# Window attention on one core: three output tiles finished in one step, one exponential a step earlier, one key tile on VectorE, the input load behind the value spreading

## The chip, the core and the metric

The kernel runs on one core of one Trainium2 chip. The time is the device time of one whole execution in microseconds (us), and the median of several runs is compared. TensorE (PE in the profile), VectorE (DVE), ScalarE (ACT), GpSimd (POOL) and SyncE (SP, which here only issues DMAs) each run their own queue strictly in order and wait for each other through semaphores.

## The reference

```
x = x + L0(_gn(x))     # input (16, 56, 56, 192); _gn: mean and variance over a group of 6 channels
x = x + L1(_gn(x))

L0: a = softmax((x @ W_attn + b_attn) as (6 heads, 9 taps)); v = x @ W_v + b_v
    y = sum over the 9 taps of the 3x3 patch of v * a;  return y @ W_proj + b_proj
L1: roll by (-3, -3), cut into 7x7 windows (8 rows of 8 windows per image), 49 tokens each
    q, k, v = tokens @ qkv_weight.T + qkv_bias     # 12 heads of 16 channels
    attn = softmax(q * 16**-0.5 @ k.T + rpb + mask)
    out = (attn @ v) @ proj_weight.T + proj_bias;   roll back
```

All arithmetic is float32 apart from the weights of L0's taps, which are split into bf16 parts.

## The kernel before

Two images lie side by side on the 128 partitions: their 2 x 192 channels are three tiles, j = 0, 1, 2. A hardware loop runs over the 8 pairs of images. One turn of it first does L0 in 7 chunks of 8 image rows and then L1 in 8 **window rows** w = 0 to 7. A window row has 392 tokens per image and is worked in four **steps** p = 0 to 3, each of two windows per image. The change touches only the window rows. Nothing schedules them but the hand-written order in which each engine's `window_row` calls its parts, with the semaphores between them.

In step (w, p) the engines do this, where D is the running number of a step:

- **PE**: `turn_probs` turns the probabilities of step D (L731). `between` does half of a projection (for row w+1 the queries in step 0 and the keys in step 1; in step 2 the output projection of row w-1; in step 3 the values of window half 1 of row w+1, L695 to L699) and turns. `scores` (L718) makes the scores of step D+2, two steps ahead. `attend` (L754) multiplies the probabilities of step D by the values. `after` begins the next projection; after step 2 that is `window_values(w+1, 0)`. It writes banks R0 and R1, and R1 is where the third tile of the output projection lay, so it waits with `pe.wait_ge(fin_ok, ONE + T * (R - 1) + 3)` until DVE has read that tile.
- **DVE**: `window_row` calls, in this order, one extra part, then `prob_sum` for both halves m = 0, 1 of step D+1 (sum L1545, reciprocal L1548), then `ahead`: `score_bias` (L1531) and `score_max` (L1538) of the two halves of step D+2 and between them `keep_y` (L1553). The extra part is `finish` (L1563: output tile = PSUM + residual, into `fin`) for tiles 0 and 1 in step 2, and for tile 2 in step 3, which also copies the three columns that wrap round (L1568, here called the wrap copy). In steps 0 and 1 it is `stat_x` (L1282) on two tiles and one tile of the next image.
- **ACT**: `early`, then `keep_probs` of the two halves (L1129), `exp_step` of both halves of step D+1 (L1121), then `late`. `early` and `late` empty PSUM: queries L1096, keys L1103 and L1104 (each tile twice, for even and odd heads), values L1114, outputs L1136, turned input L964. The values of half 0 of row w+1 are emptied in `early` of step 3, and PE waits for them (`vs_kept`) before half 1.
- **POOL**: `shift_step` (subtract the maximum, L1776) twice, one staging part (L1762 or L1769), `normalize_step` (L1783) twice, a second staging part in some steps.
- **SP**: in row w the stores of row w-2, then the wait for `x_turned` and the `load` of an input chunk, then `spread` of the values of row w+1, halves 0 and 1: DMAs that lay the values out in `vbd` (L300). `attend` of steps 0 and 2 waits for them (`v_in`).

Rows 0 and 7 have an order of their own (`early`, `late`, `between`, `after` with w == 0, and `last_row`).

Of the kernel before, what the change touches and what calls it, by code (L numbers as in the profile page):

```python
# [9 lines left out]
ALU = mybir.AluOpType  # L10
# [3 lines left out]
B, H, W, C = 16, 56, 56, 192  # L14
# [78 lines left out]
def mixer(nc, x, wa, ba, wv, bv, wp, bp, wqkv, bqkv, wo, bo, table, sel_in, gmat_in, mask_in, out):  # L93
    ctx = ExitStack()
    with ctx:
# [50 lines left out]
        def plan(start, *buffers):  # L146
            made = []
            for name, shape, dt in buffers:
                made.append(nc.alloc_sbuf_tensor_at(name, shape, dt, offset=start))
                size = 2 if dt == BF16 else 4  # L150
                for n in shape[1:]:
# [46 lines left out]
        q_mm = sem("q_mm"); q_kept = sem("q_kept"); k_mm = sem("k_mm"); k_kept = sem("k_kept")  # L198
# [11 lines left out]
                   k_mm, k_kept, vv_mm, vs_kept, *v_in, sc_mm, t_add, t_max, t_sub, p_exp, p_sum, p_rec,  # L210
# [18 lines left out]
        def _(sp):  # L229
# [56 lines left out]
            with sp.Fori(0, NP) as i:  # L286
# [30 lines left out]
                for w in range(NW):  # L317
                    if w >= 2:
                        for t in range(NT):
                            store(w - 2, t)  # L320
                    if 1 <= w and w + 1 < CHUNKS:
                        sp.wait_ge(x_turned, ONE + T * (CHUNKS * (i + 1) + w))
                        load(w + 1)
                    if w < NW - 1:
                        spread(w + 1, 0)
                        spread(w + 1, 1)
# [10 lines left out]
        def _(pe):  # L337
# [138 lines left out]
            with pe.Fori(0, NP) as i:  # L476
# [225 lines left out]
                def scores(w, p):  # L702
# [6 lines left out]
                    elif p == (2 if w == 0 else 0):  # L709
                        pe.wait_ge(q_kept, ONE + T * (NW * i + w + 1))  # L710
                        pe.wait_ge(k_kept, ONE + T * (NW * i + w + 1))
                    for n in range(T):
# [103 lines left out]
                def after(w, p):  # L816
# [21 lines left out]
                    elif p == 1:  # L838
                        pe.wait_ge(k_kept, ONE + T * (R + 1) + 2)
                        begin_out(w - 1, freed=(k_kept, ONE + T * (R + 2)))  # L840
# [110 lines left out]
        def _(act):  # L951
# [81 lines left out]
            with act.Fori(0, NP) as i:  # L1033
# [65 lines left out]
                def keep_keys(w, n, bank, lo=0):  # L1099
# [5 lines left out]
                       ).then_inc(k_kept, 1)  # L1105
# [36 lines left out]
                def early(w, p):  # L1142
# [10 lines left out]
                    elif p == 1:  # L1153
                        keep_keys(w + 1, 0, ROW_BANKS[0])
# [34 lines left out]
                def window_row(w):  # L1189
                    for p in range(PAIRS):  # L1190
# [4 lines left out]
                        exp_step(w1, p1, 0)  # L1195
                        exp_step(w1, p1, 1)
                        late(w, p)

                def last_row():
# [5 lines left out]
                    keep_probs(w, 0, 1)  # L1205
                    keep_next(w, 0, Y_BANK)
                    keep_next(w, 1, R0)
                    exp_step(w, 1, 0)
                    keep_next(w, 2, R1)
                    exp_step(w, 1, 1)  # L1210
# [3 lines left out]
                    exp_step(w, 2, 0)  # L1214
# [48 lines left out]
                for n, bank in enumerate((R0, Y_BANK, R1)):  # L1263
                    keep_queries(0, n, bank, EDGE)
                for m in range(2):
# [6 lines left out]
        def _(dve):  # L1272
# [117 lines left out]
            with dve.Fori(0, NP) as i:  # L1390
# [132 lines left out]

                def score_bias(w, p, m):
# [32 lines left out]
                def finish(w, n, bank):  # L1557
# [7 lines left out]
                    if n == T - 1:  # L1565
                        dve.wait_ge(fin_ok, ONE + T * (R + 1))
                        wrap = lambda c: fin[:, :, c:c + RT].rearrange("p j (r n) -> p j r n", n=W)[:, :, :, 0:SHIFT]
                        nc.vector.tensor_copy(wrap(0), wrap(W)).then_inc(fin_wrap, 1)  # L1568
# [12 lines left out]
                def window_row(w):  # L1581
                    for p in range(PAIRS):
                        w1, p1 = pair_after(w, p, 1)
                        if w >= 1 and p == 2:
                            finish(w - 1, 0, ROW_BANKS[0])
# [287 lines left out]
```

## Time and profile before

| | us |
|---|---|
| median of 3 runs (3870.67 to 3879.84) | 3873.07 |
| the profiled execution | 3867.02 |
| its span | 3865.2 |
| PE busy | 3398.0 (88%) |
| DVE busy | 2706.8 (70%) |
| POOL busy | 2293.2 (59%) |
| ACT busy | 1874.1 (48%) |
| mean granted TensorE clock, as a share of full speed | 0.928 |

The profile is of one execution. A wait is idle time of an engine just before an instruction, put down to the event that came last. The chain of work that ended last runs 49% of the span through PE, 12% through ACT, 11% through DVE and 11% through DMAs.

### The profile page before, as it was taken

Reading aid. Unit: us, or ns where it says so; the run is one execution under the profiler, and the core shown is the slowest. Engines: PE = TensorE matmul, PEld = TensorE weight load, DVE = VectorE, ACT = ScalarE, POOL = GpSimd, SP = SyncE. Lnnn points to the kernel's source line nnn. Section 1 sums busy time; section 2 is a strip of 40 time slices with the busy share of each in tenths; the row PEclk is TensorE's granted clock in tenths of the full one; section 3 lists DMA queues with packets and bytes.
Section 4 is the critical chain, followed back from the end, with each engine's and each line's share of the span. In section 5 each row is a group of like instructions: output and inputs, shape, how many; then the busy total and the mean of one; then the engine's idle time right before and its main releaser. Section 6 shows DMA issues by size and latency. Waiting matters only on the chain.

```text
span 3865.2 us, 105389 instructions
## 1 busy us (share of the span) xinstructions
PE 3398.0 (88%) x39908; PEld 2047.9 (53%) x39908; DVE 2706.8 (70%) x4465; ACT 1874.1 (48%) x3602; POOL 2293.2 (59%) x1889
## 2 busy tenths in 40 slices
PE   6988889888898888988889888898889988899888
PEld 3456644566445664455644566445663466634655
DVE  5966669666795667956678567786668766687665
ACT  3444544555435544355543555445554455544555
POOL 3765547665475654756547655566555666466664
PEclk7999989999998989999999999999989999899898
DMA  4722237221461223612246112561215512164121
GB/s 106 143 63 63 70 70 140 58 79 56 89 136 41 80 61 86 133 52 69 72 92 130 52 55 73 103 123 49 73 54 121 111 44 79 53 131 97 53 68 59
DMA packets 204343, 317.51 MB, mean 82 GB/s; under 512 B 16922, under 2 KB 176154, under 8 KB 203802
## 3 DMA queue, kind: packets, MB, share of 16 engines
q0 software_dynamic: 31936, 148.66, 19.7%
q1 hardware_dynamic: 171866, 161.61, 14.2%
q8 instruction: 343, 5.62, 0.6%
q14 instruction: 198, 1.62, 0.1%
HBM read 45.97 MB, written 38.54 MB: 22 GB/s over the span
## 4 chain that ended last, share of the span: by engine, by line
PE 49%; ACT 12%; issue 11%; DMA 11%; DVE 11%; POOL 3%; SPq 2%; DVEq 0%; ACTq 0%; POOLq 0%
PE P L699 7%; DMA prod<-prod 6%; PE P L731 6%; DMA vbd<-vs 5%; PE P L695 3%; PE P L654 3%; PE P L488 3%; PE P L656 3%; PE P L754 3%; DVE sp__70 L1531 3%; ACT pt L1129 3%; ACT sp__70 L1121 3%; PE P L718 2%; ACT kbd L1104 2%; ACT kbd L1103 2%
## 5 line engine op out<-in xcount | busy, mean ns | idle before, releaser
L1783 POOL TENSOR_TENSOR sp__70<-sp__70,rc 128x588 f32<-128x588 f32 x512 | 589.9, 1173 | 829.6 <-DVE rc L1548 829.6
L1427 DVE TENSOR_TENSOR prod<-P,vpad 128x896 f32<-128x896 f32 (+1 forms) x768 | 791.2, 1050 | 131.0 <-PE P L488 120.1
L1545 DVE TENSOR_REDUCE sm<-sp__70 128x12 f32<-128x588 f32 x512 | 377.9, 738 | 710.0 <-ACT sp__70 L1121 706.0
L1776 POOL TENSOR_TENSOR sp__70<-sp__70,mx 128x588 f32<-128x588 f32 x512 | 598.3, 1173 | 165.6 <-DVE mx L1538 158.0
L488 PE MATMUL P<-at,sel 108*128 108x448 bf16 x1512 | 426.5, 361 | 61.3 <-DVE prod L1427 30.9
L1531 DVE TENSOR_TENSOR sp__70<-P,relb 128x588 f32<-128x588 f32 x512 | 383.8, 750 | 88.4 <-PE P L718 88.4
L1129 ACT ACTIVATE pt<-P 98x588 f32<-98x588 f32 x512 | 313.3, 659 | 233.9 <-PE P L731 227.8
L1696 POOL DMA_DIRECT2D prod<-prod x216 | 202.3, 941 | 358.6 <-DVE prod L1427 355.1
L731 PEld LDWEIGHTS P<-ident,sp__70 113*98 113x98 f32 x3072 | 357.1, 141 | 94.9 <-issue 34.9
L731 PE MATMUL P<-ident,sp__70 113*98 113x113 f32 x3072 | 384.9, 281 | 25.0 <-DVE sp__70 L1531 24.0
L1538 DVE TENSOR_REDUCE mx<-sp__70 128x12 f32<-128x588 f32 x512 | 389.5, 761 | 9.3
L1114 ACT ACTIVATE vs<-P 98x192 f32<-98x192 f32 x512 | 140.6, 329 | 424.5 <-PE P L699 422.7
L488 PEld LDWEIGHTS P<-at,sel 108*128 108x128 bf16 x1512 | 113.2, 98 | 430.7 <-issue 236.7
L1121 ACT ACTIVATE sp__70<-sp__70 128x588 f32<-128x588 f32 x512 | 329.0, 695 | 0.1
L1712 POOL TENSOR_TENSOR psum_p<-psum_p,prod 128x1344 f32<-128x1344 f32 x96 | 302.3, 3149 | 5.9 <-DVE prod L1427 2.0
L695 PE MATMUL P<-wt,xw 64*98 64x192 f32 x512 | 140.7, 405 | 167.5 <-DVE fin L1563 157.4
L754 PE MATMUL P<-pt,vbd 98*32 98x49 f32 x12288 | 209.4, 214 | 66.4 <-DMA vbd<-vs 33.2
L699 PE MATMUL P<-wt,xw 128*98 128x192 f32 x1024 | 260.4, 411 | 0.0
L718 PE MATMUL P<-kbd,qs 32*64 32x98 f32 x12288 | 231.9, 262 | 22.0 <-ACT pt L1129 14.3
L754 PEld LDWEIGHTS P<-pt,vbd 98*32 98x32 f32 x12288 | 178.3, 113 | 118.0 <-issue 112.5
L1039 ACT ACTIVATE xa<-P,bias 128x448 f32<-128x448 f32 x168 | 107.5, 640 | 256.3 <-PE P L506 217.2
L699 PEld LDWEIGHTS P<-wt,xw 128*98 128x98 f32 x1024 | 199.2, 207 | 49.6 <-issue 40.7
(256 smaller groups left out, 7308.9 us busy)
## 6 DMA issues: line engine op xcount, KB each, us to landing
prod<-prod POOLq DMA_DIRECT2D x216, 672.0 KB, 5.5
vbd<-vs SPq DMA_DIRECT2D x512, 147.0 KB
xin<-in_x SPq DMA_DIRECT2D x126, 336.0 KB, 4.1
out<-ot SPq DMA_DIRECT2D x184, 168.0 KB, 4.0
out<-ot SPq DMA_DIRECT2D x80, 84.0 KB
wn<-in_L_conv_qkv_weight SPq DMA_DIRECT2D x2, 432.0 KB, 6.3
wno<-in_L_conv_proj_weight SPq DMA_DIRECT2D x2, 144.0 KB, 7.4
self<-in_sel SPq DMA_DIRECT2D x3, 91.1 KB
```

Source lines behind the costliest of these rows:

```text
L488: last = mm(P[:, 2 * (n % 2) + b, 0:CT], sel[:, k, :], at[:, col:col + CT], start=True, stop=True)
L699: last = mm(out_of(bank, p), src[:, j, tok(p)], wt[:, j, v], start=False, stop=(p == 1))
L731: last = turn(P[0:2 * N, 2 * m + g // 4, g % 4 * 2 * SLOT:g % 4 * 2 * SLOT + QUERIES], sp_[0:QUERIES, (2 * p + m) % SOFTS, g * 2 * N:(g + ...
L754: last = mm(P[32 * r:32 * r + 32, Y_BANK, col:col + N], vbd[w % 2][:, 2 * p + half, image, 2 * HD * g:2 * HD * (g + 1)], pt[:, m, g, half, ...
L1121: go(sp_[:, b, :], sp_[:, b, :], ACT.Exp).then_inc(p_exp, 1)
L1129: go(pt[:, m, :, :, :].rearrange("p g h n -> p (g h) n"), src, ACT.Copy).then_inc(p_kept, 1)
L1427: tt(by_row(dst), by_row(P[:, b:b + len(op), 0:CT]), val, ALU.mult).then_inc(prod_ok, 1)
L1531: tt(by_bank(sp_[:, b, :]), P[:, 2 * m:2 * m + 2, 0:T * 2 * N].rearrange("p r (n k) -> p r n k", n=T), by_bank(relb[:, kind, :]), ALU.add) ...
L1538: red(mx[:, b, :], sp_[:, b, :].rearrange("p (h k) -> p h k", h=NH), AX.X, ALU.max).then_inc(t_max, 1)
L1545: red(sm[:, b, :], sp_[:, b, :].rearrange("p (h k) -> p h k", h=NH), AX.X, ALU.add).then_inc(p_sum, 1)
L1776: tt(per_head(sp_[:, b, :]), per_head(sp_[:, b, :]), spread(mx[:, b, :]), ALU.subtract).then_inc(t_sub, 1)
L1783: tt(per_head(sp_[:, b, :]), per_head(sp_[:, b, :]), spread(rc[:, b, :]), ALU.mult).then_inc(p_norm, 1)
```

## The change

Nothing that is computed changes. Five orders do:

- DVE: all three `finish` calls stand in step 2, behind `prob_sum` of half 0; the wrap copy is a part of its own, `wrap_out`, in step 3; `stat_x` takes all three tiles in step 0; every extra part stands between the two `prob_sum` calls.
- DVE instead of ACT empties the first of the three key tiles of rows 2 to 7 (`first_keys_kept`), between the two `prob_sum` calls of step 1. A new semaphore `k_first` tells PE, which waits for it at `scores` of step 0 of a row and before `begin_out`.
- ACT: the exponential of half 0 of a step is issued at the end of the step before the one in which it stood, behind `late`. That of half 1 stays behind `keep_probs`.
- POOL: `normalize_step` of half 0 stands before the staging part.
- SP: the two `spread` calls stand before the wait for `x_turned` and the `load`.

```diff
@@ sync
+                    if w < NW - 1:
+                        spread(w + 1, 0)
+                        spread(w + 1, 1)
                     if 1 <= w and w + 1 < CHUNKS:
                         sp.wait_ge(x_turned, ONE + T * (CHUNKS * (i + 1) + w))
                         load(w + 1)
-                    if w < NW - 1:
-                        spread(w + 1, 0)
-                        spread(w + 1, 1)
@@ tensor: scores
                         pe.wait_ge(k_kept, ONE + T * (NW * i + w + 1))
+                        if w > 1:
+                            pe.wait_ge(k_first, ONE + (NW - 2) * i + w - 1)
@@ tensor: after, p == 1
                         pe.wait_ge(k_kept, ONE + T * (R + 1) + 2)
+                        pe.wait_ge(k_first, ONE + (NW - 2) * i + w)
                         begin_out(w - 1, freed=(k_kept, ONE + T * (R + 2)))
@@ scalar: keep_keys
-                       ).then_inc(k_kept, 1)
+                       ).then_inc(k_kept, 2 if w > 1 and n == 1 else 1)
@@ scalar: early
-                    elif p == 1:
-                        keep_keys(w + 1, 0, ROW_BANKS[0])
@@ scalar: window_row
                         w1, p1 = pair_after(w, p, 1)
-                        exp_step(w1, p1, 0)
                         exp_step(w1, p1, 1)
                         late(w, p)
+                        w2, p2 = pair_after(w, p, 2)
+                        exp_step(w2, p2, 0)
@@ scalar: last_row
+                    exp_step(w, 1, 1)
                     keep_next(w, 0, Y_BANK)
                     keep_next(w, 1, R0)
-                    exp_step(w, 1, 0)
                     keep_next(w, 2, R1)
-                    exp_step(w, 1, 1)
+                    exp_step(w, 2, 0)
                     keep_probs(w, 1, 0)
                     keep_probs(w, 1, 1)
-                    exp_step(w, 2, 0)
                     exp_step(w, 2, 1)
@@ vector
+                def first_keys_kept(w):
+                    dve.wait_ge(k_mm, ONE + T * (NW * i + w) + 1)
+                    for e in range(2):
+                        last = ts(kbd[:, w % 2, 0, e, :], P[:, R0, 0:RT], me[:, e:e + 1], kb[:, 0, e:e + 1],
+                                  ALU.mult, ALU.add)
+                    last.then_inc(k_first, 1)
@@ vector: window_row
                         w1, p1 = pair_after(w, p, 1)
-                        if w >= 1 and p == 2:
-                            finish(w - 1, 0, ROW_BANKS[0])
-                            finish(w - 1, 1, ROW_BANKS[1])
+                        prob_sum(w1, p1, 0)
+                        if w >= 1 and p == 1:
+                            first_keys_kept(w + 1)
+                        elif w >= 1 and p == 2:
+                            for n in range(T):
+                                finish(w - 1, n, ROW_BANKS[n])
                         elif w >= 1 and p == 3:
-                            finish(w - 1, 2, ROW_BANKS[2])
+                            wrap_out(w - 1)
                         elif w >= 2 and p == 0:
-                            stat_x(i + 1, w - 2, (0, 1))
-                        elif w >= 2:
-                            stat_x(i + 1, w - 2, (2,))
-                        prob_sum(w1, p1, 0)
+                            stat_x(i + 1, w - 2, range(T))
                         prob_sum(w1, p1, 1)
                         ahead(w, p)
@@ gpsimd: window_row
                             shift_step(w1, p1, 1)
+                            normalize_step(w1, p1, 0)
...
                         if w1 < NW:
-                            normalize_step(w1, p1, 0)
                             normalize_step(w1, p1, 1)
```

**DVE, from the end of step 2 into step 3 of a middle row, before:** P is PSUM, `sp__70` the scores, `relb` the bias, `mx` the maxima, `yt` the attended values, `fin` the output row, `xr` the residual.

```order
L1531 TENSOR_TENSOR sp__70<-P,relb 128x2x3x98
L1537 ISA
L1538 TENSOR_REDUCE mx<-sp__70 128x12
L1531 TENSOR_TENSOR sp__70<-P,relb 128x2x3x98
L1552 REGISTER_ALU
L1553 COPY yt<-P 128x3x98
L1537 REGISTER_ALU
L1538 TENSOR_REDUCE mx<-sp__70 128x12
L1560 REGISTER_ALU
L1563 TENSOR_TENSOR fin<-P,xr 128x8x7x7
L1568 COPY fin<-fin 128x3x7x3
```

DVE, step 2 of the same row in the changed kernel, whose line numbers are 10 higher (`sm` are the sums, `rc` their reciprocals):

```order
L1555 TENSOR_REDUCE sm<-sp__70 128x12
L1558 RECIPROCAL rc<-sm 128x12
L1570 REGISTER_ALU
L1571 REGISTER_ALU
L1573 TENSOR_TENSOR fin<-P,xr 128x8x7x7
L1570 REGISTER_ALU
L1573 TENSOR_TENSOR fin<-P,xr 128x8x7x7
L1570 REGISTER_ALU
L1573 TENSOR_TENSOR fin<-P,xr 128x8x7x7
L1555 TENSOR_REDUCE sm<-sp__70 128x12
L1558 RECIPROCAL rc<-sm 128x12
L1540 REGISTER_ALU
```

The third output tile stood behind the whole of `ahead`; now it stands ahead of it.

ACT, from step 2 into step 3 of a middle row, before (`xa` is the input, `vs` the values, `pt` the turned probabilities):

```order
L964 ACTIVATE xa<-P 128x8x56
L963 REGISTER_ALU
L964 ACTIVATE xa<-P 128x8x56
L1109 ISA
L1110 ISA
L1114 ACTIVATE vs<-P 98x2x6x16 x2
L1109 REGISTER_ALU
L1114 ACTIVATE vs<-P 98x2x6x16 x2
L1127 REGISTER_ALU
L1129 ACTIVATE pt<-P 98x588 x2
```

ACT, the same place in the changed kernel:

```order
L967 ACTIVATE xa<-P 128x8x56
L966 REGISTER_ALU
L967 ACTIVATE xa<-P 128x8x56
L1123 ISA
L1124 ACTIVATE sp__70<-sp__70 128x588
L1112 ISA
L1113 ISA
L1117 ACTIVATE vs<-P 98x2x6x16 x2
L1112 REGISTER_ALU
L1117 ACTIVATE vs<-P 98x2x6x16 x2
L1130 REGISTER_ALU
L1132 ACTIVATE pt<-P 98x588 x2
```

An exponential now stands between the turned input and the values.

## Rows read from the trace of the kernel before

**Rows 1.** The page, busy time of each engine, share of the span, instructions.

```profile
PE 3398.0 (88%) x39908; PEld 2047.9 (53%) x39908; DVE 2706.8 (70%) x4465; ACT 1874.1 (48%) x3602; POOL 2293.2 (59%) x1889
```

**Rows 2.** Who waited for whom: total us, times, longest.

```profile
PE P L695 <- DVE fin L1563: 157.4, 48, 3.3
```

**Rows 3.** Timeline of PE, step 2 on: start, us, engine, line [idle <-releaser].

```profile
838.16 1.33 PE L731 MATMUL P<-ident,sp__70 113*98 113x113 f32 x12
...
840.00 0.82 PE L662 MATMUL P<-yt,wot 128*128 128x392 f32 x2
...
842.45 0.78 PE L754 MATMUL P<-pt,vbd 98*32 98x49 f32 x48
846.53 0.63 PE L695 MATMUL P<-wt,xw 64*98 64x192 f32 x1 [3.30 <-DVE fin L1563]
...
859.81 1.33 PE L731 MATMUL P<-ident,sp__70 113*98 113x113 f32 x12
```

**Rows 4.** Timeline of DVE in the same step 2.

```profile
838.47 0.57 DVE L1563 TENSOR_TENSOR fin<-P,xr 128x392 f32<-128x392 f32 x1
840.20 0.56 DVE L1563 TENSOR_TENSOR fin<-P,xr 128x392 f32<-128x392 f32 x1 [1.16 <-PE P L661]
...
842.68 0.72 DVE L1531 TENSOR_TENSOR sp__70<-P,relb 128x588 f32<-128x588 f32 x1
...
845.84 0.56 DVE L1563 TENSOR_TENSOR fin<-P,xr 128x392 f32<-128x392 f32 x1
```

**Rows 5.** Stretches: us, busy (x) of PE, PEld, DVE, ACT, POOL, PEclk, DMA, GB/s.

```profile
843.30:846.50 3.20, 0.00 (x0) 0.00 (x0) 3.13 (x7) 0.00 (x0) 2.63 (x3) 0.80 0.00 0
846.50:849.70 3.20, 3.17 (x13) 2.53 (x14) 0.73 (x1) 0.00 (x0) 1.35 (x2) 0.50 0.00 0
```

**Rows 6.** Timeline of PE, rows 0 and 1 of the first attention stage.

```profile
733.44 0.40 PE L695 MATMUL P<-wt,xw 64*98 64x192 f32 x1 [0.76 <-ACT kbd L1104]
...
735.65 1.33 PE L731 MATMUL P<-ident,sp__70 113*98 113x113 f32 x12
736.90 0.40 PE L695 MATMUL P<-wt,xw 64*98 64x192 f32 x1
...
773.81 0.63 PE L695 MATMUL P<-wt,xw 64*98 64x192 f32 x1 [3.30 <-DVE fin L1563]
...
777.51 1.32 PE L731 MATMUL P<-ident,sp__70 113*98 113x113 f32 x12
...
785.93 1.33 PE L731 MATMUL P<-ident,sp__70 113*98 113x113 f32 x12
```

**Rows 7.** Groups: busy, mean ns | idle just before, by releaser, whole span.

```profile
L754 PE MATMUL P<-pt,vbd 98*32 98x49 f32 x12288 | 209.4, 214 | 66.4 <-DMA vbd<-vs 33.2 <-ACT ot L1136 20.7 <-issue 2.2
...
L654 PE MATMUL P<-yt,wot 64*128 64x392 f32 x128 | 59.0, 541 | 12.3 <-ACT kbd L1104 12.3
...
L650 PE MATMUL P<-yt,wot 128*64 128x392 f32 x128 | 55.4, 514 | 9.3 <-ACT kbd L1104 9.2
```

**Rows 8.** Timeline of ACT in the step 2 of rows 3.

```profile
839.02 1.21 ACT L1129 ACTIVATE pt<-P 98x588 f32<-98x588 f32 x2 [2.54 <-PE P L731]
840.12 1.28 ACT L1121 ACTIVATE sp__70<-sp__70 128x588 f32<-128x588 f32 x2
```

**Rows 9.** Timeline of POOL, the first subtraction behind that step's scores.

```profile
844.28 1.17 POOL L1776 TENSOR_TENSOR sp__70<-sp__70,mx 128x588 f32<-128x588 f32 x1
```

**Rows 10.** Timeline of ACT, values of half 0 emptied in row 0.

```profile
735.28 1.11 ACT L1114 ACTIVATE vs<-P 98x192 f32<-98x192 f32 x4 [1.90 <-PE P L699]
```

**Rows 11.** Timeline of SP, the spreading of one row.

```profile
819.37 7.61 SPq L300 DMA_DIRECT2D vbd<-vs  x8
```

**Rows 12.** Timeline of PE, `attend` of the step 0 behind it.

```profile
827.01 0.78 PE L754 MATMUL P<-pt,vbd 98*32 98x49 f32 x48 [0.68 <-DMA vbd<-vs]
```

**Rows 13.** Timeline of DVE, the wrap copy beside POOL work and without.

```profile
846.43 0.80 DVE L1568 COPY fin<-fin 128x63 f32<-128x63 f32 x1
...
992.17 0.20 DVE L1568 COPY fin<-fin 128x63 f32<-128x63 f32 x1
```

More of the change, by code:

```diff
@@ L197, in mixer @@
         xw_first = sem("xw_first"); xw_ok = sem("xw_ok"); xr_ok = sem("xr_ok"); vs_zero = sem("vs_zero"); stage_due = sem("stage_due")
-        q_mm = sem("q_mm"); q_kept = sem("q_kept"); k_mm = sem("k_mm"); k_kept = sem("k_kept")
+        q_mm = sem("q_mm"); q_kept = sem("q_kept"); k_mm = sem("k_mm"); k_kept = sem("k_kept"); k_first = sem("k_first")
         vv_mm = sem("vv_mm"); vs_kept = sem("vs_kept"); v_in = [sem("v_in0"), sem("v_in1")]
@@ L209, in mixer @@
                    padd_ok, o_mm, x1_kept, x1_stat, x1_wrap, xw_first, xw_ok, xr_ok, vs_zero, q_mm, q_kept,
-                   k_mm, k_kept, vv_mm, vs_kept, *v_in, sc_mm, t_add, t_max, t_sub, p_exp, p_sum, p_rec,
+                   k_mm, k_kept, k_first, vv_mm, vs_kept, *v_in, sc_mm, t_add, t_max, t_sub, p_exp, p_sum, p_rec,
                    p_norm, p_turned, p_kept, y_mm, y_kept, out_mm, fin_ok, fin_wrap, ot_mm, ot_kept, *out_in]
@@ L1264, in _ @@
                     keep_queries(0, n, bank, EDGE)
+                exp_step(0, 1, 0)
                 for m in range(2):
@@ L1564, in finish, with wrap_out @@
                        by_window(xr[:, w % 2, j, :]), ALU.add).then_inc(fin_ok, 1)
[L1565 to L1568, printed above, removed]
+                def wrap_out(w):
+                    dve.wait_ge(fin_ok, ONE + T * (NW * i + w + 1))
+                    wrap = lambda c: fin[:, :, c:c + RT].rearrange("p j (r n) -> p j r n", n=W)[:, :, :, 0:SHIFT]
+                    nc.vector.tensor_copy(wrap(0), wrap(W)).then_inc(fin_wrap, 1)
                 def ahead(w, p):
@@ L1617, in last_row @@
                     finish(w - 1, 2, ROW_BANKS[2])
+                    wrap_out(w - 1)
                     prob_sum(w, 3, 0)
@@ L1631, in last_row @@
                     finish(w, 2, R2)
+                    wrap_out(w)
                 score_bias(0, 0, 0)
```

## The prediction

> **What bounds the kernel now.** I read the busy times first: PE is busy 88% of the span and no other engine over 70% [rows 1]. So a saving on PE's path counts, and work may go to the others as long as nothing on PE waits for it. The list of waits then names one wait of PE that is large and regular: the first matmul of the values (L695) waits 157.4 us in all, 48 times, for DVE's output tile (L1563) [rows 2]. 48 is six rows (1 to 6) in each of eight turns of the loop; 157.4 / 48 = 3.28 us each time.
>
> The timeline of one row shows how it arises. Step 2 begins at 838.16 on PE; `attend` starts at 842.45 and lasts 0.78, so PE is through at 843.2; the values start at 846.53 [rows 3]. The tile they wait for was complete in PSUM with L662, 840.00 + 0.82 = 840.8 [rows 3]. DVE read it only at 845.84 [rows 4]: it finished tiles 0 and 1, summed, and went through the biases and maxima of the next scores from 842.68 on. The wait is therefore one of order on DVE, not of work.
>
> The wait has a tail. In the 3.2 us in which PE is idle the granted clock is 0.80 of full, in the next 3.2 us, where PE works, it is 0.50: the lower of the two levels, 1.2 GHz [rows 5]. The matmuls behind the wait run at half speed.
>
> **The change part by part.** I sum per turn of the loop, rows 1 to 6, and multiply by eight.
>
> (a) *The third output tile in step 2.* On DVE the order becomes sum of half 0, three tiles, sum of half 1, biases. Count from PE's start of step 2, called 0. Tile 2 is in PSUM at 2.66 (840.82 - 838.16). Tiles 0 and 1 take 0.57 each and are done by 2.6 (840.20 + 0.56) [rows 4], as long as the sum of half 0 is over by about 1.5; its exponential is now issued a step earlier, so it is. Tile 2 then lies from 2.75 to 3.3. PE wants it at 5.0, so the 3.28 us go in full: 157.4 / 8 = 19.7 us per turn. What is late next on DVE? The remaining sum needs about 0.95 (the two sums fill 840.76 to 842.68) [rows 4], until 4.25; the biases started at 4.5 before. They are not late.
>
> (b) *The clock.* From the start of the values (L695) to the next row's first transposes PE needs 859.81 - 846.53 = 13.28 us in the row shown [rows 3] and 785.93 - 773.81 = 12.12 in row 1 [rows 6]. At the full clock the same work is the values half, 735.65 - 733.44 = 2.21, plus step 3, 785.93 - 777.51 = 8.42, together 10.63 [rows 6]. So the slow clock costs 1.5 to 2.65 us a row; I take the middle, 2.1, times six rows: 12.6 us. That supposes that no other gap of PE makes it fall. The waits left are under a microsecond, and [rows 12] shows one of 0.68 us, behind which the row's matmuls run at their short times.
>
> (c) *Spreading before the load.* The first spread of a row was issued at 819.37, behind a load [rows 11], although its values are read out at the start of step 3 and the load stood for a turn made at that step's end (the step lasts 8.4 us) [rows 6]. `attend` then waited 0.68 us for it [rows 12], over the span 33.2 us [rows 7]. Issued some 5 us earlier, it lands before it is wanted: 33.2 / 8 = 4.1 us. The load moves back behind eight issues (7.61 us) and is wanted more than 20 us later, in step 2 of the next row.
>
> (d) *One key tile to DVE, one exponential out of the way.* ACT loses two key activations ahead of `keep_probs` in step 1 and an exponential ahead of `late`, 0.64 us (1.28 for two) [rows 8]. PE's waits for ACT in steps 0 and 1 were 20.7 us for `ot` (attend) and 9.2 + 12.3 us for `kbd` (L650, L654) [rows 7], together 42.2, or 5.3 per turn. The activations that are waited for stand behind what ACT loses, over 1.5 us of it in step 1, and the single waits were shorter than that (48 for `kbd`, about 0.5 or less each), so I count them as gone. DVE pays two PSUM reads of 392 columns, by its own rows of that size 0.57 each, in step 1, where it was idle for the exponential. PE's new wait (`k_first`, ahead of `begin_out`; behind it in the queue stand `begin_out` and with it step 2) is for two reads that begin with step 1, while `begin_out` comes behind `attend`, more than 4 us into a step (842.45 against 838.16 in step 2). I cost it at nothing; without that cover it would be 1.1 us a row.
>
> (e) *What the exponential at a step's end costs.* It waits for the subtraction, which waits for the maxima. In step 2 the biases start at 4.3, the subtraction 1.6 us later (844.28 against 842.68) [rows 4, 9], takes 1.17 [rows 9], and the exponential 0.64: it holds ACT until 7.8. Behind it now stand the values of half 0, four activations of 1.11 us together [rows 10], which could have begun 1.84 us after PE's first L695 (735.28 against 733.44) [rows 6, 10], at 6.85. They end at 8.9. PE, at 5.0 + 2.2 = 7.2 in the transposes of step 3, wants them at 8.4 (1.25 behind the transposes' start) [rows 6]. This is a new wait of 0.5 to 0.7 us, six times: 3.6 us. In the other steps the exponential is over before `keep_probs` (0.86 after a step's start, 839.02 against 838.16) [rows 3, 8] or within 0.1 us. With 0.1 for the last key tile before `begin_out` I take 4.2 us per turn; the bounds are nothing and twice that.
>
> (f) *The rest.* POOL's first normalization moves ahead of a staging part and brings the probabilities earlier; they are not what PE waits for. The wrap copy takes 0.80 us beside POOL work and 0.20 without [rows 13]. Its new place is between sums in step 3, beside subtractions: at most a POOL instruction longer, 1.17, and the output transposes want it 2 us later. Nothing. The Trainium skill, SBUF - State Buffer, section Who interferes with whom, says that such a DVE copy and a POOL instruction take a shared port pair as a whole, and the later one stands still; by that rule the copy could also hold a POOL subtraction, for 0.2 us, and the sum would be the same. Rows 0 and 7: some exponentials now stand ahead of query and value reads in row 0 (0.2 to 0.5 us twice), and in row 7 the sums come earlier by about as much. Nothing, within 1 us either way.
>
> The sum: 19.7 + 12.6 + 4.1 + 5.3 - 4.2 = 37.5 us per turn, 300 us over eight. The profiled execution took 3867.0, so 3567; the median of the runs is 6 us above it, which gives **3573**.
>
> **The rivals.**
>
> *No new waits* (the upper side of e): all gains, 41.7 x 8 = 334 us, 3540. For it: ACT is busy under half the time. Against it: its queue is in order and the chain in (e) leaves no slack.
>
> *A wait takes part of it back.* The three tiles, the sum and the biases stand so close on DVE in step 2 that a slip of one, or of the exponential ahead of them, reaches PE in each row. With 1 to 1.5 us a row more than in (e), 48 to 72 us: 3620 to 3645. For it: tile 2 has only 1 us between its arrival and the scores. Against it: POOL and DVE are busy 70% and 59% of the span [rows 1].
>
> *The clock stays low.* The long wait goes, but the new short ones, or others, keep the clock falling once a row: the 12.6 x 8 = 101 us of (b) do not come, 3674. For it: the values now follow closely on two short waits. Against it: [rows 5], where it falls only in a long stretch without any matmul. The Trainium skill, TensorE: Matmul & The Clock Gate, section HAM oscillation, tells of a kernel whose clock fell again in every pass because of a wait; by that rule the gain in (b) hangs on no long wait being left, and I leave one only in the rows 0 and 7, which are not in the sum.
>
> *Slower.* The exponentials at a step's end hold ACT in all four steps: if the subtraction is queued behind a normalization on POOL (1.17 for one such instruction) [rows 9] and then takes its own 0.64, `keep_probs`, and with it the scores and the transposes, come 1.8 us later per step, 7.2 us a row, 348 us in all against 334 gained: 3887. It decides from 1.7 us a step on. Against it: POOL's normalization of half 0 is now over before the maxima.
>
> *It does not do what it says*: if PE's wait is ended by something else at the same moment, no change, about 3870. PE had nothing else to wait for after 843.2 [rows 3].
>
> **How the numbers follow.** A measurement of this kernel tells 0.3%, 12 us, from no change. Forecast (3550 to 3600) 0.50; no new waits 0.13; part taken back (to 3655) 0.22; clock stays low 0.08; slower 0.04; no change 0.03. The range 3530 to 3655 takes in the first three, 0.85. Faster is all but the last two: 0.93; within 0.3% 0.03; slower 0.04.
>
> **What would show it.** The wait of L695 for L1563 is gone from the list; the granted clock of the whole is above 0.97 and at 1.0 through rows 1 to 6; a middle row lasts 30 to 31 us from first transposes to first transposes; `attend` no longer waits for `vbd` or `ot`; L695 in step 3 shows some 0.6 us for ACT's L1114 (now L1117). Wrong would be: a wait of PE over 1 us in a middle row, for DVE or ACT; a granted clock of 0.5 in one; or ACT idle before the exponential of half 0 while `keep_probs` could run.

## The result and the profile after

| | before | after |
|---|---|---|
| median, us, runs on the same chip | 3871.87 (4 runs, 3865.19 to 3879.84) | 3554.78 (4 runs, 3553.39 to 3557.86) |
| ratio, 95% interval | | 0.9181 [0.9163, 0.92] |
| the profiled execution, us | 3867.02 | 3553.39 |
| its span | 3865.2 | 3551.5 |
| mean granted TensorE clock | 0.928 | 0.956 |

The kernel is faster by 8.2%. The forecast was 3573, 18 us above the median, and the median lies in the range.

In the changed kernel `turn_probs` is L733 (before L731), `scores` L720 (L718), `attend` L756 (L754), `finish` L1573 (L1563), the wrap copy L1579 (L1568), `exp_step` L1124 (L1121), the values on ACT L1117 (L1114), the keys on ACT L1106 and L1107 (L1103, L1104).

The page of after, busy times (compare [rows 1]): PE goes from 88% to 93% although its busy time falls by 110 us, DVE from 70% to 78%.

```profile
PE 3288.3 (93%) x39908; PEld 1960.4 (55%) x39908; DVE 2765.5 (78%) x4561; ACT 1834.7 (52%) x3506; POOL 2305.4 (65%) x1889
```

The list of waits of after (who waited <- for whom and its line: total us, times, longest). The wait of [rows 2] is not in it, nor one of `attend` for `vbd`, nor one for `ot`. The two that are left in rows 1 to 6 are small. Of the first, 20.2 us stand in row 0, up to 2.5 at a time; in rows 1 to 6 it is 13.2 us, in 39 of the 48 rows, up to 0.51.

```profile
PE P L650 <- ACT kbd L1107: 33.4, 47, 2.5
...
PE P L695 <- ACT vs L1117: 10.8, 47, 0.3
```

The timeline of PE, one middle row of after, from its first transposes to those of the next row (compare [rows 3]: start, us, engine, line, [idle before <- releaser]):

```profile
806.19 1.32 PE L733 MATMUL P<-ident,sp__70 113*98 113x113 f32 x12
...
813.40 1.32 PE L733 MATMUL P<-ident,sp__70 113*98 113x113 f32 x12
...
817.16 0.78 PE L756 MATMUL P<-pt,vbd 98*32 98x49 f32 x48
818.28 0.51 PE L650 MATMUL P<-yt,wot 128*64 128x392 f32 x1 [0.34 <-ACT kbd L1107]
...
820.84 1.32 PE L733 MATMUL P<-ident,sp__70 113*98 113x113 f32 x12
...
822.68 0.82 PE L662 MATMUL P<-yt,wot 128*128 128x392 f32 x2
...
825.13 0.78 PE L756 MATMUL P<-pt,vbd 98*32 98x49 f32 x48
825.84 0.40 PE L695 MATMUL P<-wt,xw 64*98 64x192 f32 x1
...
828.04 1.32 PE L733 MATMUL P<-ident,sp__70 113*98 113x113 f32 x12
829.61 0.40 PE L695 MATMUL P<-wt,xw 64*98 64x192 f32 x1 [0.24 <-ACT vs L1117]
...
836.78 1.33 PE L733 MATMUL P<-ident,sp__70 113*98 113x113 f32 x12
```

The steps last 7.21, 7.44, 7.20 and 8.74 us, the row 30.6. The values behind `attend` (L695 at 825.84) follow at once; before, 3.30 us of idle stood there. Its first matmul takes 0.40 us and not 0.63.

The timeline of DVE in the same step 2 (compare [rows 4]). All three output tiles are through before the biases begin at 825.13:

```profile
821.89 0.52 DVE L1573 TENSOR_TENSOR fin<-P,xr 128x392 f32<-128x392 f32 x1
822.88 1.23 DVE L1573 TENSOR_TENSOR fin<-P,xr 128x392 f32<-128x392 f32 x2 [0.47 <-PE P L661]
824.02 0.76 DVE L1555 TENSOR_REDUCE sm<-sp__70 128x12 f32<-128x588 f32 x1
...
825.13 0.77 DVE L1541 TENSOR_TENSOR sp__70<-P,relb 128x588 f32<-128x588 f32 x1
```

**Where the time went.** I measured rows 1 to 6 of each turn of the loop in both traces, from the first transposes of row 1 to those of row 7. Before they took 220.3 to 224.4 us (mean 222.0), after 181.2 to 185.5 (mean 182.1). That is 39.9 us a turn, 319 over eight; the two profiled executions differ by 313.6. So everything came from these six rows, and the rest (L0, rows 0 and 7) is some 6 us longer. By steps, the means over the 48 rows went from 7.94, 7.91, 12.25 and 8.91 us to 7.23, 7.31, 7.24 and 8.58: five of the 6.6 us of a row came out of step 2.

The 39.9 us divide in two. Of a turn's rows 1 to 6 PE was busy for 191.3 us before and is for 176.7 now, 14.6 less for the same matmuls; it was idle for 30.7 and is for 5.4, 25.3 less. The first part is what the faster clock gave, in the main, the second is waits.

**The clock.** The stretches of one turn, in after (us, busy us (instructions) of PE, PEld, DVE, ACT and POOL, granted clock, DMA share, GB/s): row 0, rows 1 to 6, row 7 and the beginning of L0, the rest of L0 up to the next row 0.

```profile
1117.46:1150.61 33.15, 28.66 (x504) 18.94 (x503) 20.72 (x36) 17.40 (x36) 20.86 (x20) 0.90 0.18 57
1150.61:1331.88 181.27, 176.35 (x3172) 125.26 (x3170) 146.82 (x264) 109.97 (x224) 133.65 (x129) 1.00 0.26 75
1331.88:1378.87 46.99, 37.89 (x472) 24.72 (x472) 27.77 (x58) 26.40 (x48) 14.13 (x14) 0.85 0.18 53
1378.87:1550.99 172.12, 163.75 (x825) 72.58 (x822) 146.80 (x207) 71.90 (x125) 117.32 (x69) 0.96 0.60 120
```

The same row 0 and rows 1 to 6 before:

```profile
1192.63:1225.90 33.27, 28.96 (x504) 19.87 (x503) 19.90 (x36) 17.53 (x35) 20.40 (x20) 0.89 0.18 57
1225.90:1449.61 223.71, 192.31 (x3171) 137.07 (x3170) 141.70 (x255) 116.27 (x240) 133.30 (x131) 0.92 0.21 61
```

Over the whole run, the time at the lower level (1.2 GHz, 0.50 in the trace) inside rows 1 to 6 fell from 273 us to 3. Those 3 us come right behind the longest gap of PE that is left there, 2.56 us in one row (at 2115 us), which no event in the trace ends; there are two more such gaps, of 1.0 and 1.8 us. Outside them it was 284 us and is 311.

### The profile page after: what moved, and what is told of

Its sections match the earlier page's. It is cut to its first block, busy times and chain, and to the rows that moved or that the text cites. A ratio compares the mean times of both kernels' runs of the same rounds, so it can differ in the third digit from the quotient of the medians.

```text
span 3551.5 us, 105486 instructions
## 1 busy us (share of the span) xinstructions
PE 3288.3 (93%) x39908; PEld 1960.4 (55%) x39908; DVE 2765.5 (78%) x4561; ACT 1834.7 (52%) x3506; POOL 2305.4 (65%) x1889
## 4 chain that ended last, share of the span: by engine, by line
PE 47%; issue 15%; DVE 14%; POOL 12%; ACT 6%; DMA 5%; DVEq 1%; ACTq 0%; POOLq 0%; SPq 0%
POOL sp__70 L1796 5%; DVE prod L1429 5%; POOL sp__70 L1789 4%; DMA prod<-prod 4%; PE P L488 4%; PE P L720 4%; PE P L733 4%; PE P L699 3%; DVE sp__70 L1541 3%; PE P L654 3%; PE P L656 3%; PE P L650 3%; PE P L756 2%; PE P L695 2%; PE P L661 2%
## 5 line engine op out<-in xcount | busy, mean ns | idle before, releaser
L1796 POOL TENSOR_TENSOR sp__70<-sp__70,rc 128x588 f32<-128x588 f32 x512 | 599.6, 1172 | 360.1 <-DVE rc L1558 340.2
L1124 ACT ACTIVATE sp__70<-sp__70 128x588 f32<-128x588 f32 x512 | 356.3, 697 | 587.9 <-POOL sp__70 L1789 587.8
L1555 DVE TENSOR_REDUCE sm<-sp__70 128x12 f32<-128x588 f32 x512 | 390.0, 762 | 299.1 <-ACT sp__70 L1124 299.1
L733 PE MATMUL P<-ident,sp__70 113*98 113x113 f32 x3072 | 352.1, 266 | 19.2 <-DVE sp__70 L1541 19.2
L733 PEld LDWEIGHTS P<-ident,sp__70 113*98 113x98 f32 x3072 | 322.4, 131 | 80.8 <-issue 56.4
L720 PE MATMUL P<-kbd,qs 32*64 32x98 f32 x12288 | 231.8, 262 | 33.7 <-ACT pt L1132 14.9
L720 PEld LDWEIGHTS P<-kbd,qs 32*64 32x64 f32 x12288 | 181.9, 133 | 87.7 <-issue 55.9
L984 ACT ACTIVATE vpad<-P,bias 128x448 f32<-128x448 f32 x171 | 108.2, 633 | 221.7 <-PE P L414 192.4
L1725 POOL TENSOR_TENSOR psum_p<-prod 128x1344 f32<-128x1344 f32 x56 | 171.8, 3069 | 75.5 <-DMA prod<-prod 75.5
L756 PE MATMUL P<-pt,vbd 98*32 98x49 f32 x12288 | 208.8, 214 | 11.3 <-ACT pt L1132 1.7
L756 PEld LDWEIGHTS P<-pt,vbd 98*32 98x32 f32 x12288 | 176.8, 113 | 58.9 <-issue 43.7
L699 PE MATMUL P<-wt,xw 128*98 128x192 f32 x1024 | 202.8, 342 | 0.0
```

What stands on the lines that cost most here:

```text
L720: last = mm(P[half * SLOT:(half + 1) * SLOT, r, n * 2 * N:(n + 1) * 2 * N], qs[rows, w % 2, j, tok:tok + SLOT], kbd[rows, w % 2, j, :, tok ...
L733: last = turn(P[0:2 * N, 2 * m + g // 4, g % 4 * 2 * SLOT:g % 4 * 2 * SLOT + QUERIES], sp_[0:QUERIES, (2 * p + m) % SOFTS, g * 2 * N:(g + ...
L756: last = mm(P[32 * r:32 * r + 32, Y_BANK, col:col + N], vbd[w % 2][:, 2 * p + half, image, 2 * HD * g:2 * HD * (g + 1)], pt[:, m, g, half, ...
L1124: go(sp_[:, b, :], sp_[:, b, :], ACT.Exp).then_inc(p_exp, 1)
L1555: red(sm[:, b, :], sp_[:, b, :].rearrange("p (h k) -> p h k", h=NH), AX.X, ALU.add).then_inc(p_sum, 1)
L1725: tt(y0[:] if n == PADD - 1 else psum_p[:], slot(0) if n == 0 else psum_p[:], slot(k), ALU.add).then_inc(padd_ok, 1)
```

## The experiments

The kernel before was timed beside each of them: 3882.17 beside the first four, 3869.84 beside the other four. Ratios are against that. The changed kernel's 3554.78 belongs to a kernel before of 3871.87, so a difference in us between it and one of the first four experiments is some 10 us too large; the difference by ratios, in us of 3871.87, stands beside it where it matters.

**1. The third tile alone.** Kernel before; only `finish` of tile 2 moves to step 2, and the wrap copy stays in step 3.

```diff
                             finish(w - 1, 1, ROW_BANKS[1])
+                            finish(w - 1, 2, ROW_BANKS[2])
                         elif w >= 1 and p == 3:
-                            finish(w - 1, 2, ROW_BANKS[2])
+                            wrap_out(w - 1)
```

> The kernel before with one edit: DVE finishes the third output tile in step 2, right behind the other two and ahead of both sums, and the wrap copy stands alone in step 3. Theory (the wait of L695 for the third tile and the slow clock behind it are one lump, worth 19.7 + 12.6 us per turn of the loop): 258 us less, plus some 10 us because the sums, whose exponentials have not moved, now stand behind three tiles and the biases start at 5.2 instead of 4.5 us into step 2: about 3625 us, the wait of L695 for L1563 gone, clock 1.0 in the middle rows. Rival (the edits need each other: without the earlier exponential DVE is late with the biases or the sums and PE waits over 1 us a row for them): 3670 us or more, with PE waiting for L1531 or POOL's L1783 in step 3.

Measured: 3623.71 (3619.44 to 3627.16), ratio 0.933 [0.9299, 0.9362]. The wait for `fin` is gone. The theory had 3625. Rows 1 to 6 take 190.4 us a turn, 31.6 less than before. The wait itself was 19.7. PE's busy time in these rows is 178.5 us, 12.8 less: that is its tail, the clock, forecast at 12.6 in (b). And 0.9 is taken back by `attend`, whose wait for `vbd` grew from 33.2 us to 40.7. Time at 0.50 in these rows is 14 us. What the other parts of the change take away is still in its list of waits:

```profile
PE P L754 <- DMA vbd<-vs: 40.7, 38, 2.2
...
PE P L754 <- ACT ot L1136: 19.9, 39, 0.5
```

**2. The wait kept, the clock kept up.** Kernel before; PE runs 13 matmuls whose result nobody reads into the bank of tile 1, which is free, and only then waits for tile 2.

```diff
+                        pe.wait_ge(fin_ok, ONE + T * (R - 1) + 2)
+                        stay_warm(13, R2)
                         pe.wait_ge(fin_ok, ONE + T * (R - 1) + 3)
```

> The kernel before with 13 idle matmuls (bf16, 512 columns, on a bank that holds nothing) on PE ahead of the wait for the third output tile in step 2 of rows 1 to 6. The wait for the tile ends when it did; only PE is not idle in it. Theory (the matmuls behind the wait are slow because the granted clock fell in it): the clock stays at 1.0 in the middle rows and 8 x 12.6 = 101 us go, about 3772 us. Rival (the slow stretch has another cause, as weight loads or PSUM shared with DVE): 3870 us, and the values of step 2 and the transposes of step 3 take as long as before.

Measured: 3785.92 (3776.43 to 3787.34), ratio 0.9743 [0.9709, 0.9778]. That is 96 us less than the kernel before beside it; the theory had 101. Rows 1 to 6 take 210.7 us a turn, 11.3 less (90 us), although the wait for `vbd` grew here too, from 33.2 us to 47.8, 1.8 a turn. So some 60% of the gap's cost were the gap, 40% its tail. Timeline of PE, at the place of [rows 3], and the granted clock over it (columns as in [rows 5]; it was 0.80 and 0.50 there):

```profile
829.43 2.98 PE L377 MATMUL P<-sel,identb 108*128 108x512 bf16 x13
...
832.76 0.40 PE L695 MATMUL P<-wt,xw 64*98 64x192 f32 x1 [0.36 <-DVE fin L1565]
```

```profile
825.00:835.00 10.00, 9.57 (x146) 6.53 (x145) 7.08 (x13) 3.64 (x8) 6.90 (x7) 1.00 0.00 0
```

The values still start as late as the third tile lets them, but L695 takes 0.40 us as in an undisturbed row and not the 0.63 of [rows 3].

**3. The exponentials back in their old place.** Changed kernel; in the middle rows the edit is this, in row 0 and the last row the exponentials go back likewise.

```diff
                         w1, p1 = pair_after(w, p, 1)
+                        exp_step(w1, p1, 0)
                         exp_step(w1, p1, 1)
                         late(w, p)
-                        w2, p2 = pair_after(w, p, 2)
-                        exp_step(w2, p2, 0)
```

> The changed kernel with ScalarE's exponentials back as before (both halves behind keep_probs), all else as changed. Theory (the earlier exponential is what lets DVE sum half 0 ahead of the tiles and the keys): in step 2 the first sum comes at 2.6 us, the tiles end at 5.3, the second sum at 6.3 and the biases at 8.5 instead of 6.5, so PE waits about 1.3 us a row, 48 rows: about 3617 us. Rival (the exponential at a step's end costs PE its 0.23 us wait before the values and gives nothing): 3544 us.

Measured: 3727.33 (3724.18 to 3730.95), ratio 0.9602 [0.957, 0.9635]: 172 us slower than the changed kernel (163 by ratios), where the theory said 62 more and the rival 11 less. It is also 104 us slower than experiment 1, which moved the tile alone: without the early exponential the other orders cost more than they bring. Steps 0, 1, 2 of a middle row last 8.46, 8.11 and 8.62 us in place of 7.22, 7.44 and 7.20. Its list of waits has three that the changed kernel lacks or has small (that for `sp__70` is 19.2 us there, 20 times):

```profile
PE P L733 <- DVE sp__70 L1540: 84.8, 110, 1.8
...
PE P L382 <- DVE fin L1572: 57.4, 48, 1.3
...
PE P L650 <- DVE kbd L1529: 19.6, 48, 0.7
```

Timeline of DVE in step 0 of a middle row of this kernel, and the PE instruction that waits:

```profile
769.03 0.77 DVE L1554 TENSOR_REDUCE sm<-sp__70 128x12 f32<-128x588 f32 x1 [2.52 <-ACT sp__70 L1124]
...
769.98 1.65 DVE L1283 BATCH_NORM_STATS2 stats<-xa 128x6 f32<-128x448 f32 x3
771.55 0.75 DVE L1554 TENSOR_REDUCE sm<-sp__70 128x12 f32<-128x588 f32 x1
...
772.47 0.72 DVE L1540 TENSOR_TENSOR sp__70<-P,relb 128x588 f32<-128x588 f32 x1
```

```profile
774.80 0.40 PE L733 MATMUL P<-ident,sp__70 113*98 113x113 f32 x2 [1.08 <-DVE sp__70 L1540]
```

DVE is idle for 2.52 us at the head of its queue, for the sum of half 0. The three statistics, or the key tile, or the output tiles, stand behind that sum, and the biases behind them. In the order of the changed kernel the exponential of half 0 is a step ahead, so this head wait is short (0.41 us at 820.94 in step 2), and the extra part lies in the time in which DVE would wait for half 1. The exponential's place is what allows the sum to stand ahead of the extra part.

**4. The third tile back in step 3.** Changed kernel with tile 2 finished in step 3, ahead of the sums.

```diff
+                        if w >= 1 and p == 3:
+                            finish(w - 1, 2, ROW_BANKS[2])
                         prob_sum(w1, p1, 0)
...
                         elif w >= 1 and p == 2:
-                            for n in range(T):
-                                finish(w - 1, n, ROW_BANKS[n])
+                            finish(w - 1, 0, ROW_BANKS[0])
+                            finish(w - 1, 1, ROW_BANKS[1])
```

> The changed kernel with the third output tile back in step 3 (behind the biases and maxima of step 2), all else as changed. Theory (the tile is nearly the whole of the gain): the wait of 3.3 us and the slow clock behind it come back in rows 1 to 6, 258 us more, about 3813 us, clock about 0.93. Rival (the shorter chain of the other parts hides part of the wait): under 3750 us.

Measured: 3780.53 (3779.03 to 3786.22), ratio 0.9743 [0.971, 0.9776], 226 us above the changed kernel (218 by ratios). The theory had 258 more, 3813 us, and the rival under 3750: the result lies between them. All else in the change is worth 2.6% of the time before by itself, some 100 us. Alone, the two parts so gave 258 (experiment 1) and 102, together 360, and the whole gave 317: some 40 us are given by either. Part of that is seen here, where the wait for the third tile is shorter than before (147.5 us against 157.4) and so is the low clock behind it (232 us against 273). The wait is back and with it the clock: 232 us at 0.50 in rows 1 to 6, and the granted clock of the whole is 0.932.

```profile
829.98 0.63 PE L695 MATMUL P<-wt,xw 64*98 64x192 f32 x1 [3.06 <-DVE fin L1573]
...
834.19 2.17 PE L733 MATMUL P<-ident,sp__70 113*98 113x113 f32 x12
```

The twelve transposes behind it take 2.17 us where they take 1.32 elsewhere.

**5. The first key tile back on ACT.** Changed kernel; `keep_keys(w + 1, 0, ROW_BANKS[0])` is in `early` of step 1 again, `first_keys_kept` and its waits are gone.

```diff
+                    elif p == 1:
+                        keep_keys(w + 1, 0, ROW_BANKS[0])
...
-                        if w >= 1 and p == 1:
-                            first_keys_kept(w + 1)
```

> The changed kernel with the first key tile back on ScalarE, ahead of keep_probs of step 1, all else as changed. Theory (it delays ScalarE's chain in step 1: keep_probs from 0.86 to 1.65 us into the step, the output activation and both other key tiles by 0.3 to 0.9): PE waits about 0.9 us a row more in step 1, 48 rows, 43 us: about 3598 us. Rival (PE would wait for the output row or the scores anyway): 3555 us.

Measured: 3571.01 (3565.48 to 3574.06), ratio 0.9222 [0.9206, 0.9238]. The keys' move is worth 16 us, 0.4%, not the 43 of the theory. Only 8 of them lie in rows 1 to 6, which take 183.2 us a turn, 1.0 more; the rest lies where the move changes little, and I can't assign it. Step 1 goes from 7.44 to 7.62. The wait of the second half of the key projection for ACT is back, and that of the first is not larger than in the changed kernel:

```profile
PE P L650 <- ACT kbd L1104: 26.4, 48, 2.5
...
PE P L654 <- ACT kbd L1104: 12.2, 48, 0.3
```

`keep_probs` of step 1 does come late as the theory has it, 1.54 us into the step, but little on PE waits for it. ACT has the room (it works 53% of the span here), and with the exponential of half 0 out of the way at a step's start the two activations cost little.

**6. The load ahead of the spreading.** Changed kernel with SP's old order.

```diff
+                    if 1 <= w and w + 1 < CHUNKS:
+                        sp.wait_ge(x_turned, ONE + T * (CHUNKS * (i + 1) + w))
+                        load(w + 1)
                     if w < NW - 1:
                         spread(w + 1, 0)
                         spread(w + 1, 1)
```

> The changed kernel with the input load and its wait ahead of the spreading again, all else as changed. Theory (the first spread of a row is issued some 5 us later and attend of step 0 waits for it as before, 0.7 to 1.3 us in 37 to 40 rows): about 33 us more, 3588 us, with a wait of attend for vbd of about 33 us in all. Rival (transfers land early enough in either order): 3555 us.

Measured: 3592.92 (3579.12 to 3594.57), ratio 0.9268 [0.9248, 0.9288]: 38 us slower than the changed kernel (34 by ratios; the theory had 33). Rows 1 to 6 take 187.6 us a turn, 5.5 more; step 0 lasts 8.1 us in the mean instead of 7.2. The wait of `attend` is back:

```profile
PE P L756 <- DMA vbd<-vs: 39.4, 40, 2.2
```

It lists 4.9 us a turn. This is term (c), 4.1, and a little more. The wait has a tail as well: rows 1 to 6 spend 17 us at 0.50 here, 3 in the changed kernel. The clock fell behind five of the seven waits of 1.67 to 2.18 us in these rows, and behind none of the seven of 1.0 to 1.4.

**7. The values ahead of the exponential.** Changed kernel; the exponential of half 0 that stands at the end of step 2 is issued behind the values of half 0 in step 3.

```diff
                         early(w, p)
+                        w1, p1 = pair_after(w, p, 1)
+                        if w >= 1 and p == 3:
+                            exp_step(w1, p1, 0)
                         keep_probs(w, p, 0)
                         keep_probs(w, p, 1)
-                        w1, p1 = pair_after(w, p, 1)
                         exp_step(w1, p1, 1)
                         late(w, p)
                         w2, p2 = pair_after(w, p, 2)
-                        exp_step(w2, p2, 0)
+                        if w < 1 or p != 2:
+                            exp_step(w2, p2, 0)
```

> The changed kernel with one exponential moved: that at the end of step 2 stands behind the values of half 0 in step 3 (rows 1 to 6), ahead of keep_probs. Theory (the wait of 0.23 us for L1117 before the values of half 1 is the price of the exponential's place, 47 times, 10.8 us, and the exponential still comes in time): 3544 us, that wait gone. Rival (keep_probs is then later by the exponential and the scores or the transposes of step 0 with it): no gain or a loss, 3555 us or more.

Measured: 3531.27 (3529.13 to 3539.2), ratio 0.9119 [0.9104, 0.9134]: 24 us less than the changed kernel, where the theory said 11. The wait of L695 for the values is not in its list; step 3 lasts 8.42 us (831.66 to the row's start before it at 823.24) instead of 8.74:

```profile
823.24 1.32 PE L733 MATMUL P<-ident,sp__70 113*98 113x113 f32 x12
824.49 0.40 PE L695 MATMUL P<-wt,xw 64*98 64x192 f32 x1
...
831.66 1.33 PE L733 MATMUL P<-ident,sp__70 113*98 113x113 f32 x12
```

**8. That, and the last key tile's first half ahead of the last output.** In `late` of step 1 the activation for the even heads of tile 1 goes ahead of `keep_out`, the other stays behind it.

```diff
+                        keep_keys(w + 1, 1, ROW_BANKS[1], part=0)
                         if w >= 2:
                             keep_out(w - 2, 3, Y_BANK)
-                        keep_keys(w + 1, 1, ROW_BANKS[1])
+                        keep_keys(w + 1, 1, ROW_BANKS[1], part=1)
```

> e7's kernel with a second edit: on ScalarE in step 1 the first of the two activations of the second key tile stands ahead of the last output activation instead of behind it. Theory (begin_out's wait of 0.34 us for that tile, 47 times, is ScalarE's order; the output activation is still in time for attend): 16 us less than e7, 3528 us. Rival (attend now waits for the output activation by as much as begin_out gains): as e7, 3544 us.

Measured: **3515.62** (3509.55 to 3527.98), ratio 0.909 [0.9069, 0.9112], the fastest of all, 39 us under the changed kernel (35 by ratios) and 16 under experiment 7, as the theory had it; the interval lies clear of its [0.9163, 0.92]. Step 1 lasts 6.97 instead of 7.44. The wait of L650 is left only in row 0:

```profile
PE P L650 <- ACT kbd L1110: 20.2, 8, 2.5
```

```profile
804.45 1.32 PE L733 MATMUL P<-ident,sp__70 113*98 113x113 f32 x12
...
808.28 0.78 PE L756 MATMUL P<-pt,vbd 98*32 98x49 f32 x48
808.99 0.54 PE L650 MATMUL P<-yt,wot 128*64 128x392 f32 x1
...
811.42 1.33 PE L733 MATMUL P<-ident,sp__70 113*98 113x113 f32 x12
```

In experiments 7 and 8 the steps were shortened by more than the wait that the list shows (0.32 us against 0.24, 0.47 against 0.34). The starts show why. A wait is counted from the end of the matmuls before it, but without a wait the next matmul starts 0.07 us ahead of that end. L695 follows the start of the transposes by 1.25 us in experiment 7 and by 1.57 in the changed kernel: 0.32. L650 follows the start of `attend` by 0.71 us in experiment 8 and by 1.12 in the changed kernel: 0.41. The rest of the 0.47 is a gap too short for the list, ahead of L654 (0.94 us after L650 in the changed kernel, 0.81 in experiment 8), less 0.07 by which `attend` starts later in its step.

## Why the prediction was right, point by point

The mechanism was right and is shown by experiments 1, 2, 4 and 6; the sum over rows 1 to 6 was 37.5 us a turn and is 39.9. The measured terms below add up to 38.8. The 1.1 left are PE's busy time, which is 1.8 less than in experiment 1 (176.7 against 178.5), less 0.7 for the gaps that no event ends. Per turn:

| term | forecast | measured | from |
|---|---|---|---|
| (a) third tile | 19.7 | 19.7 | the wait is gone |
| (b) clock | 12.6 | 12.8; 11.3 | PE's busy time, experiment 1; the rows' time, experiment 2 |
| (c) spreading | 4.1 | 4.1; 5.5 | the wait; experiment 6 |
| (d) ACT relief, less 0.6 for the last key tile | 4.7 | 3.6 | the waits listed |
| (e) values, six waits | -3.6 | -1.4; -2.2 | the wait; experiment 7 |

(a) *Right, with its working.* Tile 2 lay complete at 1.84 + 0.82 = 2.66 us from the start of step 2 (822.68 against 820.84), exactly as forecast, and was done by 3.27, in the "2.75 to 3.3" of the prediction. The biases began at 4.29 instead of 4.5.

(b) *Right.* The size, 2.1 us a row, came out at 2.1 by experiment 1 and 1.9 by experiment 2. The rival in which the clock stays low fell: short waits of up to 0.51 us remain in nearly every row, and rows 1 to 6 had 3 us at 0.50 in the whole run. Those, in one row of 48, are strictly the sign "a granted clock of 0.5 in one" that was to speak against the prediction; they follow the gap of 2.56 us, for which no event is to be seen, and not one of the waits. The Trainium skill, TensorE: Matmul & The Clock Gate, section HAM oscillation, ties such a recurring fall to a wait of the loop; experiments 2 and 4 agree, since the fall goes when the gap is filled and comes back with it. Failed, however, was the sign that the granted clock of the whole would be above 0.97: it is 0.956. I had not counted how much of the low clock lies outside the six rows. It was 284 us of 558, and nothing in the change touches it.

(c) *Right.* The load, issued at 837.49 behind eight spreads that begin at 829.66, made no new wait.

```profile
829.66 7.54 SPq L300 DMA_DIRECT2D vbd<-vs  x8
```

(d) *Right in direction, mis-sized.* I took all 42.2 us of waits for `ot` and `kbd` as gone. The 20.7 for `ot` and the 12.3 of L654 are gone, but L650 went from 9.2 to 13.2 us (33.4, of which 20.2 stand in row 0, as before). The step at fault is the last key tile, "0.1" a row, measured at 0.34 in 39 of the 48 rows, and worth 0.47 in experiment 8. Its two activations stand behind the last output's; PE's `begin_out` wants their bank as soon as `attend` is over, at 817.94, and gets it at 818.28. The timeline of ACT there:

```profile
816.42 0.48 ACT L1139 ACTIVATE ot<-P 56x384 f32<-56x384 f32 x1 [0.37 <-PE P L764]
816.81 0.67 ACT L1106 ACTIVATE kbd<-P,kb,me 128x392 f32<-128x392 f32 x1
817.37 0.67 ACT L1107 ACTIVATE kbd<-P,kb,me 128x392 f32<-128x392 f32 x1
```

The credit went to the wrong part, too: experiment 5 shows that the keys' tile on DVE brings 16 us. The 0.57 each that DVE was to pay was low; DVE's two reads of a key tile take 0.68 each, without harm.

(e) *The mechanism right, its size too large.* The exponential at the end of step 2 does hold the values, and L695 waits for them 47 times, as forecast, but 0.23 us and not 0.5 to 0.7. Timeline of ACT:

```profile
827.98 0.69 ACT L1124 ACTIVATE sp__70<-sp__70 128x588 f32<-128x588 f32 x1 [3.08 <-POOL sp__70 L1789]
828.58 0.97 ACT L1117 ACTIVATE vs<-P 98x192 f32<-98x192 f32 x4
```

The values end at 829.55, 8.71 us behind the step's start; I had 8.9. The exponential ends at 7.83; the prediction says 7.8, though its own terms add up to 7.7 (4.3 + 1.6 + 1.17 + 0.64). So that is right, but the four activations take 0.97 and not the 1.11 of row 0 [rows 10]: here all their input is ready (PE's L699 ended at 828.20), there they follow PE. And PE wants them at 8.45 rather than 8.4 (1.25 behind the transposes at 7.20, as experiment 7 shows).

(f) *Rest.* Right that it is nothing: the wrap copy does not get longer but shorter, 0.14 us. Not foreseen in any part was what the exponential's move buys (163 to 172 us in experiment 3). The prediction had only costs for it in (e) and a relief of ACT in (d). It did not change the sum, because (a) supposed the early exponential ("so it is" over by 1.5 us) and costed the orders together.

Of the other rivals: "no new waits" (3540) is nearer to the result than the forecast is, 15 us below against 18 above; the result lies between them, as (e) at half its size would have it. "A wait takes part back" and "slower" fell: in the middle row shown PE waits twice, 0.34 and 0.24 us, and for nothing else. The slower case asked for `keep_probs` to come 1.7 us late per step; in this row the exponential was over before it in steps 1 and 2, where ACT then waited for PE. In step 3 it did delay it, with the values behind it: `keep_probs` began at 1.38 us (829.42 against 828.04) instead of 0.86, and PE did not wait for it. One slip of the text: against "a wait takes part back" it gives POOL 70% and DVE 59% of the span; by [rows 1] DVE is the one with 70%. DVE was the engine at issue, so the argument is weaker than it reads.

## What to carry to other kernels

Where the bounding engine waits once in each pass, add to the wait what its matmuls behind it lose to the lower clock: here 19.7 us of waiting carried another 13. If the wait can't be removed, filling it with idle matmuls got that second part alone. A helper that waits at the head of its in-order queue hides nothing that stands behind it; put the producer a step earlier first, and then the extra work between the two halves. Look afterwards at what the moved instruction now stands in front of: the two largest waits left in rows 1 to 6 were both of that kind, and moving one exponential and one activation gave about 1% more.

## What the runs showed of the hardware

- Idle matmuls kept the granted clock at 1.0: 13 of bf16 with 512 columns, 2.98 us together, in a gap of 3.3 us; with the gap empty it was 0.80 and then 0.50 [rows 5]. Rows 1 to 6 of that run have 17 us at 0.50, against 273 before. That cheap filler alone gave 2.6% of the run.
- The wrap copy, 63 columns of f32 on 128 partitions, took 0.80 us in 48 of its 64 cases before and 0.14 in 48 of them after; in the other 16 it took 0.20 both times, with POOL idle. All its executions after (min / median / max ns, first and last start):

```profile
L1579 DVE COPY fin<-fin x64: 137/139/205, 300.1 to 3545.5; 128x63 f32<-128x63 f32 x64
```

In the row shown it starts at 829.66, as POOL's subtraction ends (828.50 + 1.17 = 829.67) and before the normalization, which waits for the reciprocal on DVE:

```profile
828.50 1.17 POOL L1789 TENSOR_TENSOR sp__70<-sp__70,mx 128x588 f32<-128x588 f32 x1 [0.55 <-DVE mx L1548]
829.82 1.17 POOL L1796 TENSOR_TENSOR sp__70<-sp__70,rc 128x588 f32<-128x588 f32 x1 [0.15 <-DVE rc L1558]
```

Before, it started 0.42 us into a POOL subtraction (846.43 [rows 13]) and ended at 847.23, 0.06 us behind that subtraction's end, as in all 48 cases:

```profile
846.01 1.17 POOL L1776 TENSOR_TENSOR sp__70<-sp__70,mx 128x588 f32<-128x588 f32 x1 [0.55 <-DVE mx L1538]
```

The Trainium skill, SBUF - State Buffer, section Who interferes with whom, says that a copy on DVE in a mode that uses both of its port pairs and a POOL instruction exclude each other for a whole instruction, and that the one that comes first goes first; these times agree, and the new place is one in which POOL is between two instructions. No experiment moved the copy alone, but two show that its time goes with its place: in experiment 1 it starts 0.16 us ahead of a subtraction in those 48 and takes 0.19 to 0.20 us in all 64, and in experiment 4, with the third tile back, it still takes 0.14 in 48.
- DVE reads 392 columns of f32 out of PSUM in 0.50 to 0.57 us with a second tensor as operand (L1573, [rows 4]) and in 0.68 with two per-partition scalars (L1530, 662 to 685 ns in 96 executions).
